# Gated attention block: query deviation folded behind the scores, new order of gate sums, centres and residual

## The reference

```python
def _mlstm_head(q, k, v, ig, fg):                 # 8 heads of 64
    cs = cumsum(log_sigmoid(fg)), a leading 0
    log_D = where(ltr, cs - cs.T, -inf) + ig.T
    D = exp(log_D - max_log_D)
    C = (q @ k.T / 8) * D
    normalizer = maximum(abs(C.sum(-1)), exp(-max_log_D))
    return C / (normalizer + 1e-6) @ v
xn = layernorm(x)
ig, fg = concat([xn, ctx, ctx]) @ igate_kernel + bias, ... @ fgate_kernel + bias
h = heads of _mlstm_head(xn, ctx, ctx, ig, fg); h = h * rsqrt(mean(h**2) + 1e-6) per head
x = x + tanh(g_xattn) * h
t = act_quant(layernorm(x))                        # round(t * 127 / max|t|) per token
g, u = t @ ternary(w_gate).T, t @ ternary(w_up).T  # 512 -> 2048
h = relu(g)**2 * u
x = x + tanh(g_ffn) * act_quant(h) @ ternary(w_down).T
```

## Time and profile before

| | |
|---|---|
| median of 3 runs | 601.32 us (600.64 to 601.65) |
| profiled execution | 600.03 us, its span 598.3 us |
| busy: PE, DVE, ACT, POOL | 565.5, 525.9, 452.9, 129.4 us |
| granted TensorE clock, mean | 0.994 |
| moved by transfers | 62.68 MB |

### The profile page before, as it was taken

The page is one execution under the profiler, slowest core; times in us unless marked ns, Lnnn a source line. Parts: engine busy times, 40 slices in busy tenths (PEclk is TensorE's granted clock), DMA queues, the critical chain, the costliest instruction groups (busy, mean ns, idle before and its releaser), DMA issues.

```text
span 598.3 us, 18337 instructions
## 1 busy us (share of the span) xinstructions
PE 565.5 (95%) x6506; PEld 339.5 (57%) x6587; DVE 525.9 (88%) x1151; ACT 452.9 (76%) x926; POOL 129.4 (22%) x284
## 2 busy tenths in 40 slices
PE   8986679999999999999999999999999999999997
PEld 4744435656565655656565665656565565656454
DVE  4799898989989898998989898998989899897965
ACT  4799889686876869687786868687786868777563
POOL 3267142130301212120221213020121212021100
PEclk9999989999999999999999999999999999999999
DMA  8968050050605023050503205050502305030001
GB/s 302 383 237 300 23 175 22 28 187 3 213 0 194 18 84 127 18 193 0 199 13 140 72 31 181 0 211 0 194 18 89 122 18 194 3 107 2 19 36 36
DMA packets 44257, 62.68 MB, mean 105 GB/s; under 512 B 1864, under 2 KB 25920, under 8 KB 44224
## 3 DMA queue, kind: packets, MB, share of 16 engines
q1 hardware_dynamic: 44224, 62.24, 29.5%
HBM read 53.72 MB, written 8.51 MB: 104 GB/s over the span
## 4 chain that ended last, share of the span: by engine, by line
PE 79%; ACT 8%; DVE 6%; issue 5%; POOL 1%; DMA 1%; SPq 0%; DVEq 0%; ACTq 0%; POOLq 0%
PE gb L1226 16%; PE ub L1226 16%; PE yb L1252 16%; PE tp L1273 8%; PE ab L1260 7%; PE ab L1240 4%; PE tp L1300 3%; PE ab L1283 3%; PE ab L1261 2%; ACT wdT L531 1%; ACT wgT L539 1%; POOL stage L449 1%; PE ab L1334 1%; ACT relu L549 1%; DVE stage L816 1%
## 5 line engine op out<-in xcount | busy, mean ns | idle before, releaser
L1226 PE MATMUL gb<-wgT,xqT 128*128 128x512 bf16 x486 | 126.9, 381 | 4.0 <-issue 3.9
L1226 PE MATMUL ub<-wuT,xqT 128*128 128x512 bf16 x492 | 127.2, 380 | 1.6 <-DVE stage L816 0.3
L1252 PE MATMUL yb<-wdT,stage 128*128 128x512 bf16 x466 | 112.0, 383 | 6.7 <-ACT stage L561 3.4
L547 ACT ACTIVATE relu<-gb 128x512 f32<-128x512 f32 x128 | 75.2, 587 | 46.0 <-PE gb L1226 45.6
L816 DVE TENSOR_TENSOR stage<-relu,ub 128x512 f32<-128x512 f32 x128 | 86.8, 678 | 15.7 <-ACT relu L549 15.5
L1226 PEld LDWEIGHTS ub<-wuT,xqT 128*128 128x128 bf16 x512 | 49.2, 98 | 62.6 <-DVE stage L816 4.7
L549 ACT ACTIVATE relu<-relu 128x512 f32<-128x512 f32 x128 | 80.7, 631 | 4.1
L943 DVE SCALAR_TENSOR_TENSOR dmat<-ab,dmat 128x384 f32<-128x384 f32 x128 | 65.1, 549 | 18.7 <-POOL dmat L457 13.0
L1252 PEld LDWEIGHTS yb<-wdT,stage 128*128 128x128 bf16 x496 | 45.9, 98 | 50.7 <-ACT stage L561 3.5
L1226 PEld LDWEIGHTS gb<-wgT,xqT 128*128 128x128 bf16 x512 | 45.9, 100 | 45.0 <-issue 1.0
L457 POOL TENSOR_SCALAR_AFFINE_SELECT dmat<-dmat 128x256 f32<-128x256 f32 x128 | 55.5, 461 | 58.8 <-ACT dmat L607 46.7
(11 more groups left out here) (139 smaller groups left out, 899.5 us busy)
## 6 DMA issues: line engine op xcount, KB each, us to landing
dmat<-max_rows SPq DMA_DIRECT2D x15, 1024.0 KB, 5.0
values<-in_ctx_v SPq DMA_DIRECT2D x16, 520.0 KB, 7.6
xs<-in_x SPq DMA_DIRECT2D x16, 512.0 KB, 5.8
cT<-in_ctx_t SPq DMA_DIRECT2D x16, 512.0 KB, 6.8
out<-stage SPq DMA_DIRECT2D x31, 256.0 KB, 2.0
stage<-in_w_gate SPq DMA_DIRECT2D x4, 1024.0 KB, 13.0
stage<-in_w_up SPq DMA_DIRECT2D x4, 1024.0 KB, 13.4
stage<-in_w_down SPq DMA_DIRECT2D x4, 1024.0 KB, 6.6
```

The source lines that it names most:

```text
L547: nc.scalar.activation(relu[:, c % 2, :], gb[c % 2][:, :], ACT.Relu).then_inc(g_free, 1)
L1226: last = nc.tensor.matmul(bank[c % 2][:, :], xqT[par][:, t, d, :], w[:, d, c * CH:(c + 1) * CH], start=(d == 0), stop=(d == KD - 1))
L1252: done = nc.tensor.matmul(yb[:, :], hqT[:, c, :], wdT[:, c, :], start=(c == 0), stop=(c == KF - 1))
```

## The change

From batch 3 on the queries are no longer normalised before the scores. SP loads x already transposed (`x_t`, made on the host like ctx_t) into qT. TensorE transposes the mean column, broadcast to 128 columns, into yb (`mean_rows`), and VectorE subtracts this row of means from qT (`centre_queries`); `q_columns`, its eviction on ScalarE and `attention_norm` remain for batches 0 to 2 only. The missing factor 1/deviation is made up elsewhere: scores and weights of the heads come out larger by the deviation, so GpSimd multiplies the floor exp(-max) by it (`normaliser_floor`, also the 1e-6), and the gate products of the queries go into columns of their own, which VectorE scales by 1/deviation in `gates_in`. ScalarE makes the deviation (`std`).

On VectorE `gates_in` stands ahead of the square sums, which are taken one half before and one half after `log_forget`; the first residual stands ahead of output(b-1, 1); hidden(b, 1, 1) stands ahead of the token maxima. From batch 2 on the token centres are made on ScalarE, negated, after `hidden_cols(b, 0)`, which now always stands ahead of them. `keep_warm(6)` becomes `keep_warm(19)`. The diff, cut to its core:

```diff
+            def turned(n, par):
+                sp.dma_start(qT[par][:, :, :], x_t[bass.ds(n, 1), :, :].rearrange("o (k p) s -> p (o k) s", p=P)).then_inc(xt_in[par], 16)
+
             def load(n, par):
                 for t in range(T):
                     sp.wait_ge(x2_ready[t], n - 1)
                 queries(n, par)
+                if not at(n, 2):
+                    turned(n, par)
                 keys(n, par)
                 padded_values(n, par)
...
+            def normaliser_floor(n, npar):
+
+                gp.wait_ge(std_ready, n - 1)
+                gp.wait_ge(enm_ready, n + 1)
+                alone(gp, gp_passed)
+                spread = std[npar][:, :, None].to_broadcast([P, T, NH])
+                nc.gpsimd.tensor_tensor(enm[npar][:, :, :], enm[npar][:, :, :], spread, ALU.mult).then_inc(floor_ready, 1)
+                nc.gpsimd.tensor_scalar(floor_eps[:, :], std[npar][:, :], NORM_EPS, 0.0, ALU.mult, ALU.add).then_inc(floor_ready, 1)
...
-            def attention_rstd(m):
+            def attention_rstd(m, par):
                 act.wait_ge(stat_step, STAT_K * m + 4)
                 rstd_of(mv[:, :, 1], lnv[:, :], rstd[:, :], rstd_step, RSTD_K * m)
+                if at(m, 2):
+                    nc.scalar.activation(std[par][:, :], lnv[:, :], ACT.Copy, scale=0.0, bias=1.0).then_inc(std_ready, 1)
+                elif not at(m, 0, 1):
+                    nc.scalar.activation(std[par][:, :], lnv[:, :], ACT.Exp, scale=0.5).then_inc(std_ready, 1)
+
+            def token_centres(n, npar):
+
+                act.wait_ge(ln2_step, LN2_K * n + 4)
+                for t in range(T):
+                    nc.scalar.activation(xm[:, t, :], x2[npar][:, t, :], ACT.Identity, scale=-1.0,
+                                         bias=mv2[:, t, 0:1]).then_inc(centred, 1)
...
-                if m is not None:
+                if third:
                     for t in range(T):
                         columns(m, qT[par], t)
...
                     sign_weight(2, 1)
-                if m is None:
-                    hidden_cols(b, 0)
-                if n is not None:
+                hidden_cols(b, 0)
+                if n is not None:
+                    if not third:
+                        token_centres(n, npar)
                     tokens_rstd(n)
-                if m is not None:
...
+            def centre_queries(m, par):
+
+                dve.wait_ge(rows_full, m - 2)
+                dve.wait_ge(xt_in[par], turned_loads(m, par))
+                for t in range(T):
+                    half = qT[par][:, :, t * P:(t + 1) * P]
+                    mean_row = yb[:, None, t * P:(t + 1) * P].to_broadcast([P, KD, P])
+                    nc.vector.tensor_tensor(half, half, mean_row, ALU.subtract).then_inc(q_ready, 1)
+
             def gates_in(m):
 
                 dve.wait_ge(tp_full, FULL * (gate_use(m, GATES) + 1))
-                nc.vector.tensor_tensor(gates[:, :, :], tp[:, 0:T * 2 * NH].rearrange("p (t g) -> p t g", t=T),
-                                        gbias[:, :, :], ALU.add).then_inc(tp_free, 1)
+                if at(m, 0, 1, 2):
+                    nc.vector.tensor_tensor(gates[:, :, :], tp[:, 0:T * 2 * NH].rearrange("p (t g) -> p t g", t=T),
+                                            gbias[:, :, :], ALU.add).then_inc(tp_free, 1)
+                else:
+                    of_context = tp[:, 0:T * 2 * NH].rearrange("p (t g) -> p t g", t=T)
+                    of_queries = tp[:, T * 2 * NH:2 * T * 2 * NH].rearrange("p (t g) -> p t g", t=T)
+                    dve.wait_ge(rstd_step, RSTD_K * (m + 1))
+                    for t in range(T):
+                        nc.vector.scalar_tensor_tensor(gates[:, t, :], of_queries[:, t, :], rstd[:, t:t + 1], gbias[:, t, :],
+                                                       ALU.mult, ALU.add).then_inc(gate_scaled, 1)
+                    dve.wait_ge(gate_scaled, T * (m - 2))
+                    nc.vector.tensor_tensor(gates[:, :, :], gates[:, :, :], of_context, ALU.add).then_inc(tp_free, 1)
                 dve.wait_ge(tp_free, gate_use(m, GATES) + 1)
...
                 hidden(b, 0, 1)
+                if prev and m is not None:
+                    centre_queries(m, par)
                 if n is not None:
...
                 quantise_low(b, 0)
-                if n is not None:
-                    head_squares(n)
                 if not prev:
+                    head_squares(n, 0, 1)
                     weight_scale(2)
                     dve.wait_ge(winv_step, WINV[2])
                     nc.vector.scalar_tensor_tensor(wprod[:, 2:3], wmean[:, 2:3], 1.0 / 127.0, tanhs[:, 1:2],
                                                    ALU.mult, ALU.mult).then_inc(winv_step, 1)
-                if m is not None:
                     gates_in(m)
-                if n is not None:
                     mean_squares(n)
-                if m is not None:
                     log_forget(m)
+                else:
+                    if m is not None:
+                        gates_in(m)
+                    if n is not None:
+                        head_squares(n, 0)
+                    if m is not None:
+                        log_forget(m)
+                    if n is not None:
+                        head_squares(n, 1)
+                        mean_squares(n)
                 if n is not None:
                     scale_heads(n)
                 if m is not None:
                     cumulative(m, par)
+                if prev and n is not None:
+                    residual(n, npar)
                 if prev:
                     output(b - 1, 1, npar)
                 else:
                     hidden(b, 1, 0)
-                if n is not None:
                     residual(n, npar)
                 if not prev:
                     second_residual(n, npar)
...
                     hidden(b, 1, 0)
-                if n is not None:
-                    token_centres(n, npar)
+                if prev:
+                    hidden(b, 1, 1)
+                if n is not None:
+                    token_maxima(n, npar)
                 if not prev:
                     scale_weight(2, 3)
-                else:
-                    hidden(b, 1, 1)
                 if n is not None:
                     quantise_tokens(n)
...
+                    if c == 0 and m is not None:
+                        pe.wait_ge(q_ready, Q_K * (m + 1))
...
+            def mean_rows(b, m):
+
+                pe.wait_ge(stat_step, STAT_K * (m + 1))
+                pe.wait_ge(o_ready, 2 * b - 1)
+                alone(pe, pe_passed)
+                for t in range(T):
+                    last = nc.tensor.transpose(yb[:, t * P:(t + 1) * P], mv[:, t, 0:1].to_broadcast([P, P]), ident[:, :])
+                last.then_inc(rows_full, 1)
...
+                        elif at(m, 0, 1, 2):
+                            pe.wait_ge(a_free[t], column_use(m) + 1)
                         else:
-                            pe.wait_ge(a_free[t], column_use(m) + 1)
+                            pe.wait_ge(q_ready, Q_K * m + t + 1)
                     src, row = (cT[par], KD + kd) if part == 0 else (qT[par], kd)
                     width = P // tiles
+                    whole = at(m, 0, 1, 2)
+                    col = t if whole else T * part + t
                     for g in range(tiles):
-                        done = nc.tensor.matmul(tp[width * g:width * (g + 1), t * 2 * NH:(t + 1) * 2 * NH],
+                        done = nc.tensor.matmul(tp[width * g:width * (g + 1), col * 2 * NH:(col + 1) * 2 * NH],
                                                 src[:, kd, t * P + width * g:t * P + width * (g + 1)], gk[:, row, :],
-                                                start=(part == 0 and kd == 0), stop=(part == 1 and kd == KD - 1))
+                                                start=(kd == 0 and not (whole and part == 1)),
+                                                stop=(kd == KD - 1 and not (whole and part == 0)))
...
             max_columns(1)
-            keep_warm(6, ub[1])
+            keep_warm(19, ub[1])
             weight_total(1)
...
                 chunk(b, 0, 2, par)
+                if prev and m is not None:
+                    mean_rows(b, m)
                 if n is not None:
...
                     heads_out(n, 3, npar)
-                if m is not None:
+                if not prev:
                     q_columns(m, par)
                 if prev:
-                    down(b - 1, 1, 0, KF // 2)
+                    down(b - 1, 1, 0, KF // 2, m)
                 if m is not None:
...
+    laid["x_t"] = laid["x"].transpose(0, 2, 1)
```

More of the change, by code:

```diff
@@ L30, with gated_block @@
 GATE_TILES = 4
-def gated_block(nc, x, ctx_t, ctx_v, small_in, w_gate, w_up, w_down, max_rows, out):
+def gated_block(nc, x, x_t, ctx_t, ctx_v, small_in, w_gate, w_up, w_down, max_rows, out):
     B, S, D = x.shape
@@ L93, in gated_block @@
         rstd = sb("rstd", [P, T], F32)
```

(25 more changed lines are left out.)

68 lines of the change are left out of this document (40 added, 28 removed).

## The result

The changed kernel takes 621.14 us (median, 620.91 to 621.25) against 600.98 for the kernel before beside it, a ratio of 1.0334 [1.0316, 1.0351]. Its profiled execution took 620.91 us, with a span of 619.2 us against 598.3 and a mean granted clock of 0.992; it moved 69.49 MB, the 6.8 MB more being x_t.

The account below looks back on a forecast made before the run. Two bounds: TensorE and VectorE's stretch ending with hidden(b, 1, 0). Thirteen steps at 1.50 us (19.5), prologue 2.2 and step 14 0.3 make 22.0 on 600.03: 622.0, stated as 623 us, range 616 to 629.

Parts of the forecast that it names:

- over 1 us for `hidden(b, 1, 0)`: In the loop, a sign that the forecast is right: TensorE waits over 1 us for this VectorE product.
- The first rival: In the loop, TensorE alone is the bound: 13 x 1.07 = 13.9 off, 2.5 on, 589.9 us; chance 0.11.
- the rival of 649: TensorE's stalls take the granted clock down, about 2 us a step: 623 + 26 = 649 us; chance 0.04.
- To T: Loop up to T, the gates' start on VectorE: 0.45 us later a step, with T = 315.25.
- the pair of mean rows: TensorE's two added transposes of the broadcast mean, after chunk 2: 0.30 us a step, bounds 0.22 and 0.30.
- The relief of 1.07: TensorE, per step: eight q transposes go (1.37 us), two mean transposes come (0.30), net 1.07 us.
- From T to a: VectorE from the gates' start T to a: 0.45 us more delay a step, a starting at T + 4.56.
- early enough for the cumulative sum: VectorE's logf, started at T + 1.20, was to be ready in time for TensorE's cumulative sum.
- From a to hidden: VectorE from a to hidden(b, 1, 0): 0.60 us more a step, as GpSimd's second residual waits for the later output.
- the second rival: Only part of the loop chain's delay is real: +0.6 us a step, 611.6 us (606 to 616); chance 0.17.
- The prologue: Before the loop, 13 more warm products delay ScalarE's first up sign: +2.2 us, from 0 to 2.8.
- The 0.3 for step 14: In step 14 the residual swap and the centres act alone: +0.3 us (0 to 0.6).

Follow-up runs that it names:

- f3: Changed kernel with the edits of e1, e2, e4, f1 and f2, and the gates between the two square sums: 593.48 us, 0.9882 of the kernel before.
- e4: Changed kernel with the centring of the queries behind weigh 4 and 5 instead of ahead of them: 618.12 us.
- e2: Changed kernel with output(b-1, 1) again ahead of the first residual: 617.62 us.
- e3: Changed kernel with both square sums ahead of the gates again: 610.68 us.
- f1: Changed kernel with hidden(b, 1, 0) ahead of the token statistics on VectorE: 611.32 us.
- f2: Changed kernel with csum and a made ahead of the scaled heads on VectorE: 618.97 us.
- e1: Changed kernel with keep_warm(6) instead of keep_warm(19): 619.84 us.
- f7: f3 with keep_warm(19) instead of keep_warm(6): 596.57 us, 0.9934 of the kernel before.
- f5: Kernel before, without the fold, with the first residual ahead of output(b-1, 1): 603.61 us, 1.0050 of the kernel before.
- f4: Kernel before, without the fold, with hidden(b, 1, 0) ahead of the token statistics: 602.01 us, 1.0020 of the kernel before.

## Why the prediction was right, and where its terms were off

**The mechanism held.** The loop had a second bound, VectorE's stretch that ends with `hidden(b, 1, 0)`, and the change lengthened it. All marks but one that were named for "right" are there: a round of 35.59 (35.65 said), TensorE waiting 0.92 for a (0.9), VectorE held before the gates and before the second statistics pass, by TensorE and by GpSimd, and weigh 4 1.20 behind the start of the centring. The one that failed is "over 1 us for `hidden(b, 1, 0)`": it is 0.8 in the mean. The first rival, TensorE alone as the bound, needed a round under 34.15 without such waits. It was not wrong about what leaves TensorE, 1.07 said and 1.00 in f3, only about who waits for whom. The loss is the order's more than the fold's: f3 keeps the fold, changes orders and the warm products, and is faster than the kernel before. The clock held: from 338.90 to 374.50 us, one round with all the stalls, and over the loop from 111 to 575 us it was granted 1.00, so the rival of 649 was none.

**To T (0.45 said).** The gates start at 362.00 - 46.64 = 315.36, against 315.25, but by errors that nearly cancel. The fourth chunk is late by 0.47 (354.31 - 46.64 = 307.67 against 307.20), not by 0.64: the pair of mean rows costs 0.22 and not 0.30, the stall 0.27 and not 0.35 (e4). The centring starts at 304.33 instead of 304.47, weigh 4 at 305.53 instead of 305.69. Its two passes take 1.20 from start to start, as said (1.22). Against this, from the start of the gate products in the chain to the gates on VectorE it is 1.48 (360.52 to 362.00), where I had put 1.20 and 0.05. The 1.20 was the chain's length for them where nobody waited; with VectorE waiting it is 1.35. The columns of their own are not the reason: f3 has them too, and 1.23. The relief of 1.07 was near by two errors as well: the row of `down` in rows 3 has seven records for eight, so that the q transposes took 1.22 and not 1.37.

**From T to a (0.45 said).** 4.71 instead of 4.56. The two scaled products from PSUM start 0.20 apart where I had put 0.08 from two other small operations, so the sum starts at T + 0.41. The bracket of 0.62 at the scale is the uncovered Ln and Exp, 0.58 as reckoned. One thing was put at nothing and is not: logf was to be "early enough for the cumulative sum". In the changed kernel too TensorE starts that sum 0.13 after logf's end (363.64 against 363.51), and is held by 0.3. It comes to a_rows at 366.93 - 0.94 - 46.64 = 319.35 and not at 319.1, and a starts at 320.07 and not at 319.81. That its wait for a is 0.9 as said is therefore luck: both ends of it are a quarter of a microsecond late.

**From a to hidden (0.60 said): the term that was mis-sized.** 370.48 - 366.71 = 3.77 against 4.20; 3.60 before. I took GpSimd's 1.64 as the length of its pass, when it was the length beside the residual. In the changed kernel VectorE runs the scan and the first statistics pass beside it, and it takes 1.28. This is a part of the second rival, "GpSimd's pass is quicker"; it alone came true. By the starts the three terms are 0.56 + 0.60 + 0.17 = 1.33 in this round: `hidden(b, 1, 0)` at 323.84 against 322.51. The rounds alternate. In the next one the same product starts 0.19 later against its third chunk (406.13 - 384.27 = 21.86 against 370.48 - 348.81 = 21.67), and the mean of the two, 1.43, is the 1.44 of the round. So the last term is 0.17 and 0.36 in turn where 0.60 was said, and e2 gives 0.24 for it. The forecast of 1.50 hit 1.44 because 0.26 too little in the first two terms stood against 0.34 too much in the third. That is luck; with the first two as I had them and the third as measured the round would have been 35.3.

The price of each order, undone or altered alone, came out as e3 -10.5 for the gates first, f1 -9.8 for the place of hidden (which the change left as it was), e2 -3.5 for the residual, e4 -3.0 for the place of the centring, f2 -2.2, e1 -1.3 for the products. These can't be added up to the -27.7 of f3, which has another order of the square sums than e3. Of what the change did, the gates first cost most. In the sum it had no line of its own: it was spread over T and a. The largest single cause was thus in the sum but not named in it.

**The prologue (2.2 said).** Right at the place where it was reckoned, 2.16, and 2.10 and 2.23 in e1 and f7. As the price of 13 warm products for the whole kernel it was 1.3 in e1 and 3.1 between f3 and f7; the 2.2 of the sum lies between them, and the runs don't fix it better.

**Sum.** 13 x 1.44 + 2.2 = 20.9 against 22.0. The 0.3 for step 14 can't be seen. The step from 622.0 to the 623 of the forecast stood for the 1.3 by which the median before was above the profiled execution; in the changed kernel it is 0.2.

## What to carry to other kernels

When an engine is busy for 98 of 100 us, look for the second engine that finishes just in time for it: an entry of 0.3 in the waits of a weight load was that sign here. Work taken from a queue helps only if what follows in it can start sooner; with work taken away, look for the new waits in the other queue and put independent passes into them. With six warm products again, such orders turned +20 us into -7. And price a reordering with its cover: the same edit of two calls gained 2.2 us in one kernel and cost over nine in another.

## What the hardware showed that was not expected

**An addition on GpSimd has two lengths.** The same pass of 128x512 f32 takes 1.64 us in the kernel before and in e2 (1.65 in f3), where it starts just behind the start of VectorE's own addition of two SBUF tensors (365.96 for 0.68 in e2), and 1.27 or 1.28 in the changed kernel and f5, where that addition has ended. 0.36 us more for 0.5 us of overlap. Between e2 and the changed kernel, and between f5 and the kernel before, only the order of residual and output differs. The Trainium skill, "GPSIMD Engine Reference", section "Specifications", has the SBUF interfaces shared with VectorE, with contention from instructions with two SBUF inputs; the trace agrees, and these lengths are its size here.

**The clock of step 0 differs from kernel to kernel without a cause that the runs show.** From 58 to 70 us the granted clock is 0.72 in the changed kernel, 1.00 in f1 and 0.68 in f7, all with 19 warm products, and 0.86 in the kernel before, 0.81 in f3, 0.72 in f4 and 0.64 in e1, all with 6. One profile of each is too little to lay it to the count.

**Two small products from PSUM** with nothing between them but the queue start 0.20 us apart ("0.38 x2" at 362.00), where two others, which read PSUM too, start 0.08 apart.
